# Graph-attention kernel, four-head sum: VectorE does a chunk's running sums before the shares and products of the chunk that ends

## What is computed

```
x = (meta_x @ W).reshape(N, HEADS, DIM)
logits = leaky_relu(a_src[src] + a_dst[dst], 0.2)        # edges and one loop per node
ex = exp(logits - seg_max[dst])
alpha = ex / (seg_sum[dst] + 1e-16)
out = segment_sum(x[src] * alpha[:, :, None], dst)
return out.mean(axis=1) + bias
```

## Time and profile before

| | before |
|---|---|
| median of 3 runs | 10274.1 us (10271.78 to 10276.29) |
| the profiled execution | 10270.59 us |
| its span, first to last instruction | 10268.9 us |
| busy in the span | DVE 6511.5 us (63%), POOL 6508.4 (63%), PE 3047.2 (30%), ACT 2898.0 (28%) |
| mean granted TensorE clock | 0.57 of 2.4 GHz |

### The profile page before, as it was taken

How to read it: one execution, slowest core, us unless ns; L and a number is a source line. 1 busy time by engine, 2 the same in 40 slices (tenths; PEclk the granted TensorE clock), 3 DMA queues, 4 the chain that set the end, 5 groups by cost and what they waited for, 6 DMA issues and landing times. The chain is left out here.

```text
span 10268.9 us, 93901 instructions
## 1 busy us (share of the span) xinstructions
PE 3047.2 (30%) x15231; PEld 2833.1 (28%) x15231; DVE 6511.5 (63%) x19179; ACT 2898.0 (28%) x8170; POOL 6508.4 (63%) x6186
## 2 busy tenths in 40 slices
PE   3233002111116666203666444444100012222300
PEld 2132001111115666203555344444100012222200
DVE  8999877666656676203666599999323258777700
ACT  5365234333333444101333222222100012222200
POOL 2333027777767777576777667777677765555377
PEclk6665555555557887655555555555555555555555
DMA  1010361111114544213555311111111123333211
GB/s 52 16 29 28 119 203 25 25 25 25 25 26 130 160 153 151 95 43 109 174 173 176 107 45 47 49 47 42 43 45 45 42 77 95 91 93 94 77 46 39
DMA packets 455134, 791.83 MB, mean 77 GB/s; under 512 B 119921, under 2 KB 149610, under 8 KB 454558
## 3 DMA queue, kind: packets, MB, share of 16 engines
q1 hardware_dynamic: 252126, 560.13, 16.4%
q0 software_dynamic: 188448, 201.53, 9.2%
q10 hardware_dynamic: 14112, 26.10, 0.7%
HBM read 388.06 MB, written 425.04 MB: 79 GB/s over the span
## 5 line engine op out<-in xcount | busy, mean ns | idle before, releaser
L1060 POOL DMA_INDIRECT e_other<-X,e_from_rows x392 | 611.4, 1560 | 283.5 <-DVE e_fin L1361 147.2
L1738 POOL DMA_INDIRECT e_mine<-T,e_from_rows x392 | 400.8, 1022 | 570.1 <-DVE e_from_rows L1785 451.5
L743 POOL COPY sort_spare<-sort_words 128x768 f32<-128x768 f32 x272 | 369.4, 1381 | 606.9 <-DVE sort_words L802 395.7
L3407 POOL DMA_INDIRECT e4s_mine<-XA,e4s_from_rows x392 | 385.2, 983 | 477.7 <-ACT e4s_kept L3817 355.1
L2227 PE MATMUL e_turned<-ident,e_own_x 128*128 128x128 f32 x196 | 54.5, 434 | 1573.5 <-ACT e_own_x L2139 1573.5
L3428 POOL DMA_INDIRECT out_rows<-e4s_out,e4s_to_rows x392 | 386.0, 985 | 210.3 <-issue 210.3
L2375 POOL DMA_INDIRECT e_mine<-X,e_from_rows x392 | 403.8, 1030 | 174.7 <-issue 112.9
L2396 POOL DMA_INDIRECT G<-e_g_slot,e_to_rows x392 | 386.0, 985 | 181.0 <-issue 119.1
L2882 POOL DMA_INDIRECT X<-e_row,e_to_rows x392 | 422.8, 1079 | 119.4 <-issue 118.5
L3873 PE MATMUL e4s_n_result<-w_pair,e4s_n_p_t 128*128 128x128 f32 x784 | 202.0, 439 | 991.4 <-DVE e4s_n_y L3703 600.7
L1075 POOL DMA_INDIRECT X<-e_row,e_to_rows x392 | 403.4, 1029 | 141.0 <-issue 118.2
(11 more groups left out here) (708 smaller groups left out, 15940.6 us busy)
## 6 DMA issues: line engine op xcount, KB each, us to landing
XA<-e_n_xa SPq DMA_DIRECT2D x49, 1056.0 KB, 5.3
e4s_n_xa<-XA SPq DMA_DIRECT2D x49, 1056.0 KB, 6.5
X<-e_n_row SPq DMA_DIRECT2D x49, 576.0 KB
T<-pl_row SPq DMA_DIRECT2D x98, 272.0 KB
X<-e_n_row SPq DMA_DIRECT2D x49, 528.0 KB, 3.1
X<-pl_x ACTq DMA_DIRECT2D x98, 260.0 KB, 2.7
e_n_x<-X SPq DMA_DIRECT2D x49, 520.0 KB, 5.7
G<-e_n_g SPq DMA_DIRECT2D x49, 512.0 KB, 2.9
```

The lines of the kernel that those rows point to most:

```text
L1060: gp.indirect_dma_start(out=other[:, h, j, :], out_offset=None, in_=others[:, :], in_offset=bass.IndirectOffsetOnAxis(ap=from_rows[:, h, 1 ...
L1738: gp.indirect_dma_start(out=mine[:, h, j, :], out_offset=None, in_=g.T0[:, :], in_offset=bass.IndirectOffsetOnAxis(ap=from_rows[:, h, 0, j ...
```

## The change

In VectorE's `body` the call of `running_sums` for the chunk that is being added moves up: it stood behind the shares, the products and the normalised rows, and stands ahead of them. For "hyper" and "edge" nothing lies between the two places. Data, engines, sizes and semaphores stay.

```diff
                     if attending:
                         scores(attending)
+                    if adding:
+                        running_sums(adding)
                     if end and kind == "heads":
                         shares(end)
                         scaled(end, J)
                     if kind == "heads" and c[5]:
                         x3_rows(c[5], J)
-                    if adding:
-                        running_sums(adding)
                     if kind == "heads" and c[4]:
                         n, h = c[4].n, c[4].slot
```

## The result

The changed kernel takes 10313.7 us (median of 5, 10308.95 to 10320.65) against 10271.8 us (median of 5, 10269.71 to 10276.29) for the kernel before, measured beside it: ratio 1.0041 [1.0026, 1.0056], slower by 42 us. A later set of runs gave 1.0045 [1.0032, 1.0059]. The forecast was 10322 us, slower, in a range from 10304 to 10342.

The account below looks back on a forecast made before the run. VectorE was taken to bound the four-head sum, busy 92% of it. The profiled 10270.6 us plus 48 gave 10318.6; with 3.5 from profiled run to median, the forecast was 10322 us, range 10304 to 10342.

Parts of the forecast that it names:

- The place and the mechanism: Four-head sum, after a chunk's last product: L1165 waits for squares queued behind ScalarE's copies, some 75 us in total.
- Loop rounds: Four-head sum, rounds 11 to 46 without the loop's returns: L1165 comes 1.10 us later in 28 rounds, 30.8 us.
- Straight rounds: Four-head sum, rounds 4 to 10 and 47 to 49: L1165 comes 1.30 us later in each, 13.0 us.
- Round 50: Four-head sum, round without exponentials to give: L1165's wait becomes 3.48 us instead of 0.68, costing 2.8 us.
- Round 3: Four-head sum, round without squares yet: L1311 of the next round needs exponentials behind the copies, estimated 2 us (0 to 4).
- Returns of the loop: Four-head sum, 8 returns of the four-round loop: the stall there outlasts ScalarE's copies, so 0 us added.
- rival D: At the loop's returns, the stall adds to the wait instead of covering it: 9 us, 10331; no separate chance given.
- The sum: All terms of the change in the four-head sum together: 48.6 us slower, called +48 us.
- Rival A: TensorE behind the last product: its clock stays at 2.4 GHz, copies end earlier, only 19 us lost, 10293; chance 0.05.
- Rival B: GpSimd in the four-head sum: scatters stretched beside products make it the bound, +57 us more, 10380; chance 0.04.
- Rival C: L1165 to first share: a wait for exponentials goes, 29 us back; 10293 to 10300 (chance 0.07) or 10245 (0.03).

Follow-up runs that it names:

- The second pair: Kernel before and changed kernel, both unchanged, run and profiled again on one chip: 10267.4 and 10313.8 us, ratio 1.0045 [1.0032, 1.0059].

## Why the prediction was right, point by point

- **The place and the mechanism:** right. L1165 is the one instruction that waits longer, at Z + 5.06 where the working had 5.07, behind copies that end at Z + 4.37 (4.4). The forecast of the view, some 75 us of waits for the squares in all, met 71.7 us in 39 waits in the window shown.
- **Loop rounds, 28 x 1.10 = 30.8 us:** the interval from L1154 to L1165 grew by 28.8 us over them. In some rounds the clock rises midway through the transposes and L1165 comes at Z + 4.7 to 5.0. The rest of these rounds got 1.9 us shorter.
- **Straight rounds, 10 x 1.30 = 13.0:** 13.2 (9.4 in seven and 3.8 in three). **Round 50, 2.8:** 2.7. **Round 3, 2:** 2.3.
- **Returns of the loop, 0:** +0.3 in the eight intervals from L1154 to L1165, -0.2 in the rest. The stall hides the copies, and rival D is out.
- **The term that was missing:** the drain. The sum had nothing for the rounds from 51 on and for the mending; they got 4.2 us shorter. Most of that is TensorE's clock. The mending's 32 matmuls L1603 and VectorE's wait for them, first in the kernel before and then in the changed one:

```profile
7229.25 6.93 PE L1603 MATMUL e_back<-w_heads,e_z_t 128*128 128x64 f32 x32
7236.22 0.23 DVE L1154 TENSOR_TENSOR e_y<-e_back,fix_b 128x64 f32<-128x64 f32 x1 [10.49 <-PE e_back L1603]
```

```profile
7278.42 3.92 PE L1603 MATMUL e_back<-w_heads,e_z_t 128*128 128x64 f32 x32
7282.37 0.22 DVE L1154 TENSOR_TENSOR e_y<-e_back,fix_b 128x64 f32<-128x64 f32 x1 [7.48 <-PE e_back L1603]
```

  The granted clock in these matmuls was 0.50 before and 0.94 after, behind transposes at 0.50 in both. That is 3.0 us; a wait of 0.73 us for the same product in round 52 is gone as well. The second pair has the same (10.49 and 7.47 us; 0.60 gone). Why the clock rose there is not shown: TensorE's work in the 20 us ahead is alike in both kernels, and in the two runs with the sums in their old place and another order on ScalarE these matmuls ran at 0.84.
- **The sum:** 48.6 forecast, 40.8 in the stage: 2.0 from the clock in the loop, 1.9 from the rest of the loop rounds, 4.2 from the drain. Outside the stage the span grew by another 1.3. The forecast of 10322 also carried 3.5 us from the profiled execution to the median; in the changed kernel that is 1.0 (10312.7 to 10313.7), and in the kernel before it shrank to 1.2 with five runs in place of three. So the forecast was 8 us too high, 6 of them from the sum and 2.5 from that difference. The terms for the rounds hold one by one; the drain, put at nothing without a reason, is the part that the mechanism as told did not have.
- **Rival A, the clock:** half of it is true. The block behind Z does raise the clock, but behind the transposes (0.83), not during them (0.50), so the copies keep their pace. L1603's 1504 matmuls kept TensorE busy for 186.8 us; over the same rounds of the kernel before it was this row (the group by line in the stage):

```profile
L1603 PE MATMUL e_back<-w_heads,e_z_t 128*128 128x64 f32 x1505 | 333.2, 422 | 353.4 <-DVE e_y L1154 353.4
```

  That is 7.1 us a round then and 4.0 now, and none of the 146 us moved the end of a full round, since their result is needed only at the next L1154; only the drain gained by it. The Trainium skill, page "TensorE: Matmul & The Clock Gate", section "HAM oscillation", tells authors to close TensorE's gaps; here a gap was closed and the clock rose, as it says, but what the full rounds paid for was the latency of the first 4 us, which in most of them stayed at the lower level.
- **Rival B, GpSimd:** refuted. Its wait for L1361 rose from 138.6 to 184.0 us. The stretched operations changed partners: 176 of the stage's 352 gathers took 1.5 us or more before and 44 after, against 11 of 363 scatters before and 129 of 360 after: 187 stretched operations, and then 173. A scatter beside a product takes 1.90 to 2.64 us, one beside small work 0.98. These rows again speak against the inference of the Trainium skill, page "SBUF — State Buffer", section "Who interferes with whom", that descriptor generation escapes a tensor_tensor with both inputs in SBUF.
- **Rival C, time back between L1165 and the first share:** refuted. Loop rounds outside L1154 to L1165 gave 1.9 us of the 29. It also rested on a misreading: the 4.89 us of the earlier trace rows belong to the round behind a return. The four places in the loop have 4.88, 4.38, 4.72 and 4.37 us, so the difference to a straight round is 0.41 us on average and not 0.71. With the sums between the two instructions the same differences stand (15.56, 15.06, 15.45 and 15.05 against 14.86 us), though the exponentials are now there long before: they are no wait for ScalarE.

## What to carry to other kernels

Work that is moved ahead of a producer often was the cover of that producer's latency: look on the consumer's engine for the next instruction that it needs, follow the other engine's in-order queue back from there, and ask what in it can't be early. Here the queue had two jobs whose order no longer fitted. The move costs 42 us alone and gives 31 us with the other engine's queue reordered to match; the reordering without the move is a loss too (28 us between the medians, 44 in the 46 rounds). An order on one engine and an order on another are one decision; test the four combinations before you drop one.

## What was not expected of the hardware

- VectorE waits on its own semaphores, up to 1.4 us each, 27 of them in the 23.5 us named above, appeared in one run alone, and in 23 of them SP issued a store. On that chip the store's issue took some 0.7 us in up to 24 of 49 times, and never in the profiles of the other runs. The cause of the waits is open.
- Each return of the hardware loop leaves VectorE idle for about 2.9 us before its first instruction: 8 times, 22.8 to 24.0 us together in nine of the ten profiles. In the tenth, the changed kernel with the squares ahead of the exponentials, other waits before L1165 are put down to "issue" as well. No edit took it away.
- A chip can be 12% slower in other stages (11508.9 against 10267.5 us) and alike to 0.2 us in 46 rounds of this one (the version with the copies last), but not in what follows them (75.1 against 56.9 us).
